# Local blocks with probability transposes in the score banks, one front stage, and early middle norms

## The chip, the cores and the metric

The kernel runs on one core of a Trainium2 chip. The metric is the device time of one execution in microseconds. TensorE (PE) multiplies, VectorE (DVE), ScalarE (ACT) and GpSimd (POOL) compute, and SyncE (SP) issues the loads and stores. The profiler records one execution; its granted TensorE clock is a mean of the two levels 1.2 and 2.4 GHz (1.00 is 2.4).

## What is computed

Two transformer layers on x of 2 x 2048 x 128 in float32, each an attention block and a local block, both added to x under adaptive layer norms whose shift, scale and gate come from a conditioning vector:

```python
mods = silu(c) @ w_mod                      # six vectors of 128 for each layer and batch
# layer 0 attention: delta-rule memory over 4096 rows, chunks of 64, k normalised per head
# layer 1 attention: causal linear attention, 64 features, then its own feed-forward
for layer in local_block:                   # layer 0: 6 layers, 16 heads, window 32; layer 1: 2, 8, 64
    q, k, v = split(shift(x) @ Wqkv)
    q, k = rotary(l2norm(q)), rotary(l2norm(k))
    x = x + softmax(mask(8 q k'), own and previous window) v @ Wo
    a, g = split(layernorm(shift(x)) @ W1 + b1)      # 341 wide
    x = x + (a * gelu(g)) @ W2 + b2
```

The gate of the modulation is kept away from zero: magnitude at least 0.25 with its sign.

## The kernel before

The stages run one behind the other, each a block of five instruction streams (one for each engine) that wait for each other by semaphores: `zero_rows` stores two zero rows, `modulation_stage` makes `mods`, `delta_attention_stage` is the first attention, then the feed stage, `local_block_stage` for layer 0 (758 to 4124 us), `linear_block_stage` (4126 to 4330), `local_block_stage` for layer 1 (4330 to 5240) and the residual.

**The local block** works on 16 row tiles of 128 for each batch and layer: 192 tiles in layer 0 and 64 in layer 1, in a software pipeline. Every engine runs `emit(k, T, hf)` once for each half of the heads `hf`; a loop body holds two tiles, so a pair of tiles has four halves. They are called A (T even, hf 0), B (T even, hf 1), C (T odd, hf 0) and D (T odd, hf 1) here. In each half TensorE projects q and k of one tile (L1539), transposes them (L1574) and the attention output of an earlier one (L1593), projects values (L1611), transposes probabilities (L1626), writes masks (L1662) and scores (L1670) of another tile, and multiplies probabilities by values (L1691, in layer 1 L1693). Beside that, A has the up projections (L1719), of which the first parts fill gate banks and the third part factor banks; B and D the output projection (L1640) and the transpose of the input (L1650); C the feature transposes (L1703) and the down projection (L1731). ScalarE copies out of PSUM (L1808 qkT, L1816 outT, L1842 values, L1857 probabilities), and has exponentials (L1849), the gelu gates (L1914) with a table load ahead (L1928) and behind (L1933). VectorE makes softmax maxima and differences, the attention output (L1982), the rotary products and `hidden` (L2062).

The eight PSUM banks: two for projections `ps_q`, two for transposes `ps_t`, two for scores `ps_s`, two for attention outputs `ps_o`. NS is 2 in layer 0 and 1 in layer 1. Scores use columns 0 to 255 of each score bank. The probability transposes write to `ps_t[2 - NS]`; the values, feature transposes and down projection share `ps_x = ps_t[NS - 1]`, in layer 0 the other transpose bank. Waits on a count held in a register take instructions of their own on an engine's sequencer ahead of the instruction that waits.

**The front.** `modulation_stage` loads weights and vectors, makes silu, has 8 matmul calls of 384 columns, and then six VectorE operations of 128 columns for each of eight slices (L155 to L161). `delta_attention_stage` then loads x, weights and tables (L216 to L222), VectorE takes statistics of 32 tiles (L87) and roots, modulates eight groups (L99 to L103), and after the projections (L248) ScalarE copies k (L279); VectorE waits for all 32 copies and then takes squares and their sums in two parts (L310, L311).

**The linear block** has eight groups of four tiles. Its first loop does the attention and ends with `xm` (L1111), its second the feed-forward: statistics (L1053), roots, `normalise_mid` (L941 on ScalarE), transposes, `affine` (L981), up projections (L928), gelu, down projections (L918). VectorE's second loop begins three groups ahead of TensorE's.

Of the kernel before, what the change touches and what calls it, by code (L numbers as in the profile page):

```python
# [105 lines left out]
def modulation_stage(nc, mods, c_rows, w_mod):  # L106

    with ExitStack() as ctx:
        sb = lambda n, shape, dt=F32: ctx.enter_context(nc.sbuf_tensor(f"mod_{n}", shape, dt))
        sem = ctx.enter_context(stage_semaphores(nc, "mod"))  # L110
        c = sb("c", [128, 4])
        e = sb("e", [128, 4])
        silu = sb("silu", [128, 4])
        wide = sb("wide", [128, 4, 128])
        w = sb("w", [128, 2, 768])
        sign = sb("sign", [128, 128])
        mag = sb("mag", [128, 128])
        ps = [[ctx.enter_context(nc.psum_tensor(f"mod_ps{k}{j}", [128, 512], F32)) for j in range(2)] for k in range(4)]
        loaded, exped, wide_done, product, seq = sem("loaded"), sem("exped"), sem("wide_done"), sem("product"), sem("seq")
        with nc.Block() as block:  # L120
            @block.sync
            def _(sp):
                for l in range(2):
                    sp.dma_start(w[:, l, :], w_mod[l]).then_inc(loaded, 16)
                    for b in range(2):
                        sp.dma_start(c[:, 2 * l + b:2 * l + b + 1], c_rows[l][b, :].rearrange("(p o) -> p o", o=1)).then_inc(loaded, 16)

            @block.scalar
            def _(act):
                act.wait_ge(loaded, 96)  # L130
                nc.scalar.activation(e[:, :], c[:, :], ACT.Exp, scale=-1.0).then_inc(exped, 1)

            @block.tensor
            def _(pe):
                pe.wait_ge(loaded, 96)
                pe.wait_ge(wide_done, 1)
                for k in range(4):
                    for j in range(2):
                        last = nc.tensor.matmul(ps[k][j][:, 0:384], wide[:, k, :], w[:, k // 2, 384 * j:384 * j + 384], start=True, stop=True)
                last.then_inc(product, 1)  # L140

            @block.vector
            def _(dve):
                step = Steps(dve, seq)
                dve.wait_ge(exped, 1)
                step(nc.vector.tensor_scalar(e[:, :], e[:, :], 1.0, None, ALU.add))
                step(nc.vector.reciprocal(e[:, :], e[:, :]))
                step(nc.vector.tensor_tensor(silu[:, :], e[:, :], c[:, :], ALU.mult))
                nc.vector.tensor_copy(wide[:, :, :], silu[:, :].rearrange("p (k o) -> p k o", o=1).to_broadcast([128, 4, 128])).then_inc(wide_done, 1)
                dve.wait_ge(product, 1)  # L150
                for k in range(4):
                    for j in range(2):
                        src = ps[k][j]
                        out = mods[:, k, 3 * j:3 * j + 3, :]
                        step(nc.vector.tensor_copy(out[:, 0, :], src[:, 0:128]))  # L155
                        step(nc.vector.tensor_scalar(out[:, 1, :], src[:, 128:256], 1.0, None, ALU.add))

                        step(nc.vector.tensor_scalar(sign[:, :], src[:, 256:384], 0.0, 2.0, ALU.is_ge, ALU.mult))
                        step(nc.vector.tensor_scalar(mag[:, :], src[:, 256:384], -1.0, 0.25, ALU.mult, ALU.max))
                        step(nc.vector.scalar_tensor_tensor(mag[:, :], src[:, 256:384], 0.25, mag[:, :], ALU.max, ALU.max))  # L160
                        step(nc.vector.scalar_tensor_tensor(out[:, 2, :], sign[:, :], -1.0, mag[:, :], ALU.add, ALU.mult))  # L161


def delta_attention_stage(nc, x_dram, xr, mods, w_qkvT, w_oT, alpha_raw, beta_raw, tables, qkv_dram):
# [3 lines left out]
    with ExitStack() as ctx:  # L168
# [9 lines left out]
        with ExitStack() as c2:  # L178
            sb = lambda n, shape, dt=F32: c2.enter_context(nc.sbuf_tensor(f"da_{n}", shape, dt))
            ps = [c2.enter_context(nc.psum_tensor(f"da_psa{i}", [128, 512], F32)) for i in range(8)]  # L180
# [12 lines left out]
            alpha, beta = sb("alpha", [128, H]), sb("beta", [128, H])  # L193
            loaded, seq, h_ready, hT_ps, hT_done = (sem(n) for n in ("loaded", "seq", "h_ready", "hT_ps", "hT_done"))
# [17 lines left out]
            with nc.Block() as block:  # L212
                @block.sync
                def _(sp):
                    for b in range(2):
                        sp.dma_start(xr[:, 16 * b:16 * b + 16, :], x_dram[b].rearrange("(t p) d -> p t d", p=128)).then_inc(loaded, 16)  # L216
# [16 lines left out]

                @block.tensor
                def _(pe):
                    pe.wait_ge(loaded, 144)
# [899 lines left out]
def local_block_stage(nc, name, depth, heads, window, x, x_rows, mid_rows, v_rows, weights, tables):  # L1136
# [18 lines left out]
    with ExitStack() as ctx:  # L1155
# [205 lines left out]
        with nc.Block() as block:  # L1361
# [161 lines left out]
            def _(pe):  # L1523

                def project(k, T, hf, s):

                    t, h = item(T, hf, AT_PROJ)
                    if live(k, t):
                        j = NS * h + s
                        pe.wait_ge(S["xT_done"], tiles_(k, t))  # L1530
                        if s == 0:
                            pe.wait_ge(wq_in[h], reloads(k, t, 16))
# [744 lines left out]
```

## Time and profile before

| | us |
|---|---|
| median of 3 runs | 5260.22 |
| lowest and highest | 5258.66, 5263.18 |
| profiled execution | 5259.56 |
| its span | 5257.8 |
| TensorE busy in the span | 4656.7 (89%) |
| VectorE, ScalarE, GpSimd busy | 3876.4, 3195.5, 2753.1 |
| mean granted clock | 0.954 |

The profiled execution's own time is 1.8 us above its span. A time line row gives the start in us from the span's start, the length, the engine, the source line, the operation, and in brackets the idle time of the engine just before it with what ended it. Consecutive instructions of a kind are one row; matmuls in float32 appear as two each.

### The profile page before, as it was taken

The numbers are of one execution on the slowest core, as the hardware profiler recorded it, in microseconds if no ns is written. First come the engines' busy times: TensorE is split into PE (matmuls) and PEld (weight loads), VectorE is DVE, ScalarE is ACT, GpSimd is POOL, SyncE is SP. The second block draws the span as 40 slices with busy tenths as digits, with TensorE's granted clock in tenths as the row PEclk, the third lists the DMA queues.
The fourth block names the chain that finished last, engine by engine and source line by source line (L and its number), as shares of the span: only waits on it lengthen the run. The fifth ranks groups of instructions, "written<-read, shape, count | busy, mean of one in ns | idle before, by whom it ended". The sixth has DMA issues, their size and how long they took to land. (4 is left out here: it accounts for less than half of the span.)

```text
span 5257.8 us, 220614 instructions
## 1 busy us (share of the span) xinstructions
PE 4656.7 (89%) x81616; PEld 3372.6 (64%) x81616; DVE 3876.4 (74%) x8260; ACT 3195.5 (61%) x6716; POOL 2753.1 (52%) x3917
## 2 busy tenths in 40 slices
PE   3558948999999999999999999999999576999996
PEld 2556736676767666676767666767676454666665
DVE  5984567777777777777777777777777566777775
ACT  1002526677777777677777677777776344777675
POOL 0004116666666666666666666666665325555552
PEclk6996979999999999999999999999999688999998
DMA  1000125554545454555454555455554003444442
GB/s 58 17 1 18 43 57 130 137 132 134 132 130 139 127 143 127 141 131 141 128 141 128 140 131 140 129 136 133 138 134 119 17 7 87 115 113 114 114 113 77
DMA packets 704914, 564.32 MB, mean 107 GB/s; under 512 B 223492, under 2 KB 629864, under 8 KB 704008
## 3 DMA queue, kind: packets, MB, share of 16 engines
q1 hardware_dynamic: 691080, 537.36, 38.5%
q10 hardware_dynamic: 13312, 22.02, 1.3%
q14 instruction: 441, 3.61, 0.2%
q8 instruction: 81, 1.33, 0.1%
HBM read 359.38 MB, written 200.02 MB: 106 GB/s over the span
## 5 line engine op out<-in xcount | busy, mean ns | idle before, releaser
L2134 POOL TENSOR_TENSOR L_qk<-L_cos_part,L_sin_part 128x512 f32<-128x512 f32 x896 | 1128.7, 1273 | 151.5 <-DVE L_sin_part L2012 151.0
L1797 ACT ACTIVATE L_squares<-L_ps_q 128x512 f32<-128x512 f32 x896 | 534.8, 597 | 929.2 <-PE L_ps_q L1539 922.6
L1539 PE MATMUL L_ps_q<-L_w_qkv,L_xT 128*128 128x512 f32 x1792 | 971.9, 625 | 30.0 <-DVE L_sin_part L2012 11.1
L2125 POOL TENSOR_TENSOR L_qk<-L_qk,L_rnorm 128x1024 f32<-128x1024 f32 (+1 forms) x512 | 864.0, 1688 | 17.8 <-POOL L_rnorm L2108 0.5
L1574 PEld LDWEIGHTS L_ps_t<-L_ident,L_qk 128*128 128x128 f32 x3584 | 446.1, 141 | 479.1 <-issue 374.5
L2011 DVE TENSOR_TENSOR L_cos_part<-L_ps_q,L_rot 128x512 f32<-128x512 f32 x896 | 611.0, 682 | 41.2 <-POOL L_rot L2144 31.2
L2012 DVE TENSOR_TENSOR L_sin_part<-L_ps_q,L_rot 128x512 f32<-128x512 f32 x896 | 610.9, 682 | 0.0
L2013 DVE TENSOR_REDUCE L_sumsq<-L_squares 128x8 f32<-128x512 f32 x896 | 606.7, 677 | 0.0
L2102 POOL TENSOR_TENSOR L_nw_a<-L_rnorm 128x32 f32<-128x32 f32 (+1 forms) x256 | 59.5, 232 | 993.7 <-ACT L_rnorm L1827 993.7
L1574 PE MATMUL L_ps_t<-L_ident,L_qk 128*128 128x128 f32 x3584 | 540.2, 274 | 4.4 <-POOL L_qk L2125 3.2
L1808 ACT ACTIVATE L_qkT<-L_ps_t 128x512 f32<-128x512 f32 x896 | 530.6, 592 | 15.8 <-PE L_ps_t L1574 15.7
L1640 PE MATMUL L_ps_q<-L_w_out,L_outT 128*128 128x128 f32 x3584 | 446.8, 277 | 2.6 <-ACT L_outT L1816 1.7
L1626 PEld LDWEIGHTS L_ps_t<-L_ident,L_probs 128*128 128x128 f32 x2048 | 218.9, 141 | 333.7 <-issue 262.4
L1640 PEld LDWEIGHTS L_ps_q<-L_w_out,L_outT 128*128 128x128 f32 x3584 | 423.7, 193 | 4.3 <-issue 4.0
L1670 PE MATMUL L_ps_s<-L_qkT 64*32 64x64 f32 (+1 forms) x26624 | 401.8, 226 | 0.2 <-ACT L_qkT L1808 0.2
L1611 PE MATMUL L_ps_t<-L_w_qkv,L_xT 128*128 128x512 f32 x768 | 393.4, 594 | 0.6 <-issue 0.6
L1996 DVE TENSOR_TENSOR L_probs<-L_ps_s,L_neg_max 128x512 f32<-128x512 f32 x512 | 354.3, 692 | 53.6 <-DVE L_neg_max L1991 0.5
L1977 DVE RECIPROCAL L_p_rec<-L_ps_o 128x8 f32<-128x8 f32 (+1 forms) x512 | 102.9, 201 | 359.9 <-PE L_ps_o L1691 288.7
L1982 DVE TENSOR_TENSOR L_att<-L_ps_o,L_p_rec 128x512 f32<-128x512 f32 (+1 forms) x512 | 320.1, 625 | 54.3 <-DVE L_p_rec L1977 1.4
L1670 PEld LDWEIGHTS L_ps_s<-L_qkT 64*32 64x32 f32 (+1 forms) x26624 | 357.9, 107 | 0.3 <-issue 0.3
L1626 PE MATMUL L_ps_t<-L_ident,L_probs 128*128 128x128 f32 x2048 | 324.7, 281 | 28.5 <-issue 16.2
L1991 DVE TENSOR_REDUCE L_neg_max<-L_ps_s 128x8 f32<-128x512 f32 (+1 forms) x512 | 349.0, 682 | 0.2 <-PE L_ps_s L1670 0.2
(290 smaller groups left out, 8908.2 us busy)
## 6 DMA issues: line engine op xcount, KB each, us to landing
L_val<-v_rows SPq DMA_DIRECT2D x896, 260.0 KB, 3.8
v_rows<-L_val SPq DMA_DIRECT2D x384, 260.0 KB, 2.1
v_rows<-L_val SPq DMA_DIRECT2D x512, 65.0 KB, 2.0
L_rot_base<-in_rot SPq DMA_DIRECT2D x256, 128.0 KB, 2.1
v_rows<-L_val SPq DMA_DIRECT2D x128, 130.0 KB, 2.1
L_x_in<-x_rows SPq DMA_DIRECT2D x512, 32.0 KB, 1.7
mid_rows<-z SPq DMA_DIRECT2D x256, 64.0 KB, 1.6
L_f_in<-mid_rows SPq DMA_DIRECT2D x256, 64.0 KB, 2.0
```

Of the source, the lines that this page charges most:

```text
L1539: nc.tensor.matmul(ps_q[j % 2][:, :], xT[:, parity(t), :], w_qkv[:, 0:2, 256 * j:256 * j + 256], start=True, stop=True).then_inc(S["proj_p ...
L1574: last = nc.tensor.transpose(ps_t[0][:, 128 * i:128 * i + 128], qk[:, parity(t), h, s, 128 * i:128 * i + 128], ident[:, :])
L1626: last = nc.tensor.transpose(ps_t[2 - NS][:, 128 * i:128 * i + 128], probs[:, h, 128 * i:128 * i + 128], ident[:, :])
L1640: last = nc.tensor.matmul(ps_q[0][:, 0:128], outT[:, u, :], w_out[:, u, :], start=(u == 0), stop=(u == U - 1))
L1670: last = nc.tensor.matmul(S_VIEW[W * a:W * a + W, p, i, :], qkT[rows, 0, u, W + W * a:2 * W + W * a], qkT[rows, kk, u, W * a:W * a + 2 * W ...
L1797: nc.scalar.activation(squares[:, j % 2, :], ps_q[j % 2][:, :], ACT.Square).then_inc(S["sq_done"], 1)
L1808: nc.scalar.activation(dst, ps_t[0][:, :].rearrange("x (a u q) -> x a u q", a=2, u=2), ACT.Copy).then_inc(S["qkT_done"], 1)
L2011: nc.vector.tensor_tensor(R4(cos_part[:, j % 2, :]), qkp, cs[:, :, 0, :, :, :].to_broadcast([128, 2, 4, 2, 32]), ALU.mult)
L2012: nc.vector.tensor_tensor(R4(sin_part[:, j % 2, :]), qkp[:, :, :, ::-1, :], cs[:, :, 1, :, :, :].to_broadcast([128, 2, 4, 2, 32]), ALU.mul ...
L2013: nc.vector.tensor_reduce(sumsq[:, t % 2, j, :], squares[:, j % 2, :].rearrange("x (g d) -> x g d", g=8), AX.X, ALU.add).then_inc(S["ss_do ...
L2125: nc.gpsimd.tensor_tensor(v, v, r, ALU.mult).then_inc(S["normed"], 1)
L2134: nc.gpsimd.tensor_tensor(qk[:, t % 2, h, s, :], cos_part[:, j % 2, :], sin_part[:, j % 2, :], ALU.add).then_inc(S["added"], 1)
```

## The change

**Local blocks.** The probability transposes go to `P_VIEW`, columns 256 to 511 of the two score banks, and wait only for `shifted` (VectorE has read the scores), the exponentials and their values. Scores wait, ahead of the masks, for the copy of the probabilities of the same half (`pT_done`), for `att_done` and `qkT_done`, and the waits of the next half's projection are put ahead of the masks too (`ready_to_project`). Between masks and scores nothing waits, nor ahead of the weighted values, except in A for `fact_done`. In layer 0 the down projection's result goes to `ps_q[0]`, and the order in C is probability transposes, down projection, feature transposes. In layer 1 the order in C is feature transposes, probability transposes, down projection; the third part of the up projections waits for `oT_done` in place of `pT_done` (in layer 0 for `qkT_done`), and ScalarE copies the probabilities ahead of the gelu table load.

**Front.** `zero_rows` and `modulation_stage` become part of `delta_attention_stage`: its queue first loads what modulation needs, then x, weights and tables, then stores the zero rows. ScalarE copies shifts and scales (two operations of 128x1024), VectorE makes the gates in four operations of 128x1024 behind the statistics. The first part of k's squares waits for 16 copies instead of 32.

**Linear block.** Statistics, roots and `normalise_mid` of groups 0 to 2 move to turns i = 5, 6, 7 of the first loop (`EARLY_MID`); VectorE's second loop starts at group 0.

```diff
 def delta_attention_stage(...):
...
-                    act.wait_ge(loaded, 144)
+                    act.wait_ge(mod_in, 96)
+                    nc.scalar.activation(c_exp[:, :], c_in[:, :], ACT.Exp, scale=-1.0).then_inc(exped, 1)
+                    act.wait_ge(product, 1)
+                    by_part = mods[:, :, :, :].rearrange("p k (j i) d -> p (k j) i d", i=3)
+                    nc.scalar.activation(by_part[:, :, 0, :], banks[:, :, 0:128], ACT.Copy).then_inc(mods_done, 1)
+                    nc.scalar.activation(by_part[:, :, 1, :], banks[:, :, 128:256], ACT.Copy, bias=1.0).then_inc(mods_done, 1)
+                    act.wait_ge(loaded, 112)
...
+                    dve.wait_ge(x_in, 32)
                     group_stats(nc, dve, step, xr, mean, rstd, (st, mv, var, half, tmp))
+                    dve.wait_ge(mods_done, 2)
+                    raw = banks[:, :, 256:384]
+                    nc.vector.tensor_scalar(sign, raw, 0.0, 2.0, ALU.is_ge, ALU.mult).then_inc(mods_done, 1)
...
-                    dve.wait_ge(k_out, SUB)
...
                     for j in range(2):
+                        dve.wait_ge(k_out, SUB // 2 * (j + 1))
...
 def linear_block_stage(...):
...
+                    if i - 5 in EARLY_MID:
+                        normalise_mid(i - 5)
...
+                    early = i - 5
+                    if early in EARLY_MID:
+                        dve.wait_ge(S["mid_done"], early + 1)
+                        statistics(4, four(xm, early))
+                    if live(i + 1) or live(i + 3) or early in EARLY_MID:
+                        roots(0, i + 3, 0 if live(i + 1) else 4, 8 if live(i + 3) or early in EARLY_MID else 4, S["roots_a"])
...
-                for g in range(-3, NG + 1):
+                for g in range(NG + 1):
...
 def local_block_stage(...):
...
+        ps_d = ps_q[0][:, 0:256] if NS == 2 else ps_x[:, 256:512]
...
+        P_VIEW = ps_s[:, :, 256:512].rearrange("x b (i q) -> x b i q", i=2)
...
+                def ready_to_project(k, T, hf):
+
+                    t, h = item(T, hf, AT_PROJ)
+                    if live(k, t):
+                        pe.wait_ge(wq_in[h], reloads(k, t, 16))
+                        wait(pe, S["rotated"], steps_(k, t, NS * h - 2))
...
-                        wait(pe, S["pT_done"], halves(k, t, h - 1))
+                        read, g = item(T, hf, AT_SOFTMAX)
+                        if live(k, read):
+                            pe.wait_ge(S["shifted"], halves(k, read, g))
                         pe.wait_ge(S["exp_done"], halves(k, t, h))
                         for i in range(4):
-                            last = nc.tensor.transpose(ps_t[2 - NS][:, 128 * i:128 * i + 128], probs[:, h, 128 * i:128 * i + 128], ident[:, :])
+                            last = nc.tensor.transpose(P_VIEW[:, i // 2, i % 2, :], probs[:, h, 128 * i:128 * i + 128], ident[:, :])
...
-                        wait(pe, S["shifted"], halves(k, t, h - 1))
+                        v, g = item(T, hf, AT_PV)
+                        if live(k, v):
+                            pe.wait_ge(S["pT_done"], halves(k, v, g))
+                            wait(pe, S["att_done"], halves(k, v, g - 1))
+                        else:
+                            wait(pe, S["shifted"], halves(k, t, h - 1))
+                        pe.wait_ge(S["qkT_done"], steps_(k, t, NS * h + NS - 1))
                         wait(pe, S["kprev_done"], count(k, t, 1, 0))
...
-                        pe.wait_ge(consts_in, CONSTS)
-                        pe.wait_ge(S["qkT_done"], steps_(k, t, NS * h + NS - 1))
...
-                        pe.wait_ge(S["pT_done"], mine)
-                        wait(pe, S["att_done"], before)
...
                         feature_transposes(k, T)
-                        down_projection(k, T)
...
                     prob_transposes(k, T, hf)
+                    if goes_down and early:
+                        down_projection(k, T)
...
                     if goes_down and not early:
+                        down_projection(k, T)
                         feature_transposes(k, T)
-                        down_projection(k, T)
+                    ready_to_project(k, T + hf, 1 - hf)
                     scores(k, T, hf)
...
                         exponentials(k, T, hf)
+                        if NS == 1:
+                            prob_copy(k, T, hf)
                         if live(k, T - TO_UP):
                             nc.scalar.preload_act_table_set("gelu_and_others")
-                        prob_copy(k, T, hf)
+                        if NS == 2:
+                            prob_copy(k, T, hf)
```

TensorE, layer 0, the end of half B and the whole of half C, before (REGISTER_ALU is a sequencer instruction of a wait):

```order
L60 REGISTER_ALU
L1662 MATMUL L_ps_s<-L_masks,L_ident_bf 32x256 x8
L1670 MATMUL L_ps_s<-L_qkT 32x64 x32
L1691 MATMUL L_ps_o<-L_val,L_probsT 32x65 x32
L1539 MATMUL L_ps_q<-L_w_qkv,L_xT 128x512
...
L1611 MATMUL L_ps_t<-L_w_qkv,L_xT 128x512
L1626 MATMUL L_ps_t<-L_ident,L_probs 128x128 x4
L60 REGISTER_ALU
L1703 MATMUL L_ps_t<-L_ident,L_f_norm 128x128 x2
L1731 MATMUL L_ps_t<-L_w_down,L_hidden 128x128 x6
L1662 MATMUL L_ps_s<-L_masks,L_ident_bf 32x256 x8
L1670 MATMUL L_ps_s<-L_qkT 32x64 x32
```

and the same place after:

```order
L1663 REGISTER_ALU
L60 REGISTER_ALU
L1669 MATMUL L_ps_s<-L_masks,L_ident_bf 32x256 x8
L1675 MATMUL L_ps_s<-L_qkT 32x64 x32
L1698 MATMUL L_ps_o<-L_val,L_probsT 32x65 x32
...
L1614 MATMUL L_ps_t<-L_w_qkv,L_xT 128x512
L1627 MATMUL L_ps_s<-L_ident,L_probs 128x128 x4
L60 REGISTER_ALU
L1747 MATMUL L_ps_q<-L_w_down,L_hidden 128x128 x6
L60 REGISTER_ALU
L1710 MATMUL L_ps_t<-L_ident,L_f_norm 128x128 x2
L1669 MATMUL L_ps_s<-L_masks,L_ident_bf 32x256 x8
```

The probability transposes changed their bank, one more sequencer instruction stands ahead of B's masks, and the feature transposes moved behind the down projection.

ScalarE, linear block, the end of the first loop, before:

```order
L966 ACTIVATE la_low<-la_low 128x512
L954 ACTIVATE la_k_tok<-la_p_kt 128x256
L958 ACTIVATE la_attT<-la_p_t 128x512 x2
L941 ACTIVATE la_y_n<-la_xm,la_shift,la_rstd 128x128 x12
L981 ACTIVATE la_y_T<-la_p_t,la_ln 128x512
```

and after:

```order
L971 ACTIVATE la_low<-la_low 128x512
L925 ACTIVATE la_y_n<-la_xm,la_shift,la_rstd 128x128 x4
L959 ACTIVATE la_k_tok<-la_p_kt 128x256
L963 ACTIVATE la_attT<-la_p_t 128x512 x2
L932 ACTIVATE la_y_T<-la_p_t,la_ln 128x512
```

The twelve operations between the last copy of attT and the first affine are gone from there; the last four of them now stand ahead of it, the others in the two turns before.

## Rows read from the trace of the kernel before

**Rows 1.** Local blocks: stretch, length, busy PE, PEld, DVE, ACT, POOL, clock, DMA, GB/s.

```profile
758.00:4124.00 3366.00, 3261.45 (x66432) 2312.85 (x66432) 2584.73 (x5184) 2347.64 (x4799) 2135.92 (x2808) 0.99 0.50 132
...
4330.00:5240.00 910.00, 792.90 (x7985) 571.31 (x7983) 621.37 (x1462) 605.23 (x1389) 462.25 (x829) 0.97 0.38 104
```

**Rows 2.** Time line of TensorE, layer 0, half C: start us, us, engine, line, operation.

```profile
2010.97 1.02 PE L1611 MATMUL L_ps_t<-L_w_qkv,L_xT 128*128 128x512 f32 x2
2012.05 0.63 PE L1626 MATMUL L_ps_t<-L_ident,L_probs 128*128 128x128 f32 x4
...
2013.05 1.50 PE L1731 MATMUL L_ps_t<-L_w_down,L_hidden 128*128 128x128 f32 x12
2014.48 0.30 PE L1662 MATMUL L_ps_s<-L_masks,L_ident_bf 64*32 64x256 bf16 x8
...
2015.24 0.85 PE L1691 MATMUL L_ps_o<-L_val,L_probsT 64*32 64x65 f32 x64
2016.10 1.10 PE L1539 MATMUL L_ps_q<-L_w_qkv,L_xT 128*128 128x512 f32 x2
```

**Rows 3.** Time line, layer 0, half B and the start of half C.

```profile
1999.60 1.12 PE L1539 MATMUL L_ps_q<-L_w_qkv,L_xT 128*128 128x512 f32 x2
...
2005.75 0.58 ACT L1857 ACTIVATE L_probsT<-L_ps_t 128x512 f32<-128x512 f32 x1
2006.29 0.30 PE L1662 MATMUL L_ps_s<-L_masks,L_ident_bf 64*32 64x256 bf16 x8
...
2007.06 0.85 PE L1691 MATMUL L_ps_o<-L_val,L_probsT 64*32 64x65 f32 x64
2007.85 1.12 PE L1539 MATMUL L_ps_q<-L_w_qkv,L_xT 128*128 128x512 f32 x2
2009.00 0.60 ACT L1797 ACTIVATE L_squares<-L_ps_q 128x512 f32<-128x512 f32 x1 [2.33 <-PE L_ps_q L1539]
```

**Rows 4.** Time line, layer 0, the end of half A and the start of B.

```profile
2033.67 1.12 PE L1539 MATMUL L_ps_q<-L_w_qkv,L_xT 128*128 128x512 f32 x2
...
2034.38 0.69 DVE L1982 TENSOR_TENSOR L_att<-L_ps_o,L_p_rec 128x512 f32<-128x512 f32 x1
...
2035.21 0.63 PE L1593 MATMUL L_ps_t<-L_ident,L_att 128*128 128x128 f32 x4
```

**Rows 5.** Time line, layer 1, half A, then half B.

```profile
4703.19 1.13 PE L1719 MATMUL L_ps_t<-L_f_normT,L_w_up 128*128 128x256 f32 x4 [0.98 <-ACT L_probsT L1857]
...
4709.84 0.30 PE L1662 MATMUL L_ps_s<-L_masks,L_ident_bf 64*64 64x256 bf16 x4
...
4710.18 0.57 ACT L1857 ACTIVATE L_probsT<-L_ps_t 128x512 f32<-128x512 f32 x1
4710.85 0.71 PE L1693 MATMUL L_ps_o<-L_val,L_probsT 128*64 128x65 f32 x16 [0.27 <-issue]
```

**Rows 6.** Waits, layer 1, 4450 to 5150 us: total, times, longest.

```profile
PE L_ps_t L1719 <- ACT L_probsT L1857: 26.0, 27, 1.1
```

**Rows 7.** Time line of the front, 0 to 110 us.

```profile
34.20 0.29 DVE L161 SCALAR_TENSOR_TENSOR mods<-mod_sign,mod_mag 128x128 f32<-128x128 f32 x1
35.46 2.87 SPq L216 DMA_DIRECT2D xr<-in_L_attn_x  x2
...
47.31 0.87 DVE L87 BATCH_NORM_STATS2 da_st<-xr 128x6 f32<-128x128 f32 x4 [12.83 <-DMA da_beta<-in_L_attn_beta_raw]
...
63.62 1.12 DVE L99 TENSOR_SCALAR da_h<-xr,da_mean,da_rstd 128x128 f32<-128x128 f32 x4
...
109.44 2.29 DVE L310 TENSOR_TENSOR da_prod<-da_ks 128x2048 f32<-128x2048 f32 x1 [24.61 <-ACT da_ks L279]
```

**Rows 8.** Time line of the linear block, between its two loops.

```profile
4265.21 0.69 DVE L1111 TENSOR_TENSOR la_xm<-la_p_v,la_xm 128x512 f32<-128x512 f32 x1 [2.59 <-PE la_p_v L893]
...
4269.71 1.65 ACT L941 ACTIVATE la_y_n<-la_xm,la_shift,la_rstd 128x128 f32<-128x128 f32 x4 [5.75 <-DVE la_shift L1064]
...
4285.83 2.05 PE L928 MATMUL la_p_qk<-la_y_T,la_w_f 128*128 128x512 f32 x2 [13.30 <-ACT la_y_T L981]
```

More of the change, by code:

```diff
@@ L103, in modulated_group @@
     nc.vector.tensor_tensor(out, out, vec(0), ALU.add).then_inc(done, 1)
[L106 to L161, printed above, removed]
@@ L179, in delta_attention_stage @@
             sb = lambda n, shape, dt=F32: c2.enter_context(nc.sbuf_tensor(f"da_{n}", shape, dt))
-            ps = [c2.enter_context(nc.psum_tensor(f"da_psa{i}", [128, 512], F32)) for i in range(8)]
+            banks = c2.enter_context(nc.psum_tensor("da_psa", [128, 8, 512], F32))
+            ps = [banks[:, i, :] for i in range(8)]
             hT = sb("hT", [128, 4096])
@@ L235, in _ @@
                 def _(pe):
-                    pe.wait_ge(loaded, 144)
+                    pe.wait_ge(mod_in, 96)
+                    pe.wait_ge(wide_done, 1)
+                    for k in range(4):
+                        for j in range(2):
+                            last = nc.tensor.matmul(ps[2 * k + j][:, 0:384], wide[:, k, :], w_m[:, k // 2, 384 * j:384 * j + 384], start=True, stop=True)
+                    last.then_inc(product, 1)
+                    pe.wait_ge(loaded, 112)
+                    pe.wait_ge(mods_done, 6)
                     for g in range(8):
@@ L781, in linear_block_stage @@
         PHASES = NG + 5
+        EARLY_MID = range(3)
         rstd, shift = sb("rstd", [128, 2, PHASES, 8]), sb("shift", [128, 2, PHASES, 8])
@@ L1564, in qk_transposes @@
                         elif NS == 2:
-                            wait(pe, S["pT_done"], halves(k, t - 1, h - 1))
+                            wait(pe, S["qkT_done"], steps_(k, t, j - 1))
                             if hf == 1 and parity(T) == TO_UP % 2:
@@ L1587, in out_transposes @@
                         else:
-                            pe.wait_ge(S["pT_done"], halves(k, t, h))
+                            wait(pe, S["oT_done"], halves(k, t, h - 1))
                             if hf == 1 and parity(T) == TO_UP % 2:
@@ L1682, in weighted_values @@
                             wait(pe, S["fact_done"], gated)
-                        pe.wait_ge(S["pT_done"], mine)
-                        wait(pe, S["att_done"], before)
+                        s, _ = item(T, hf, AT_SCORE)
+                        if not live(k, s):
+                            pe.wait_ge(S["pT_done"], mine)
+                            wait(pe, S["att_done"], before)
                         for i in range(HU):
```

122 lines of the change are left out of this document (70 added, 52 removed).

## Prediction

> **What bounds the kernel now.** I read the busy times by stage first. Layer 0's local block takes 3366 us of the span and TensorE is busy for 3261 of them at a granted clock of 0.99; layer 1's takes 910 us with 793 busy [rows 1]. Both other engines that matter, VectorE and ScalarE, are busy for 2585 and 2348 us of the first block, so there TensorE is the engine to shorten, but only where no other engine ends the wait last. So I then read one pair of tiles as a time line. A pair has four halves: A (up projections, gelu gates), B (output projection), C (feature transposes, down projection), D (output projection). In layer 0 one pair, from half B's first projection to the next one's, is 34.07 us [rows 3, 4], and 96 pairs make the block; layer 1 has 32. A saving of 0.1 us in a pair is 10 us of the total in layer 0 and 3 us in layer 1. Last I read the front (time 0 to 110) and the seam in the middle of the linear block, where TensorE idles and a chain of other engines sets the time.
>
> **Layer 0, half C.** From the values' first matmul to the probability transposes' first stand 1.08 us [rows 2]. The two matmuls themselves need about 0.86 (0.43 each), so 0.22 is a wait: the transposes go to bank ps_t0, which ScalarE is still copying the last qkT from. Behind them the feature transposes wait for the copy of the values. From the first probability transpose to the masks pass 2.43 us for 18 small matmuls (4, 2 and 12); the 12 of the down projection alone take 1.43 with the step to the masks, at most 0.12 each, so 18 need 2.14 and 0.29 is wait. After the change the probability transposes go to the free half of the score banks, the down projection to a projection bank, and the feature transposes come last, when the values' copy is long done. Both waits go: 0.51, and I take -0.50. What is late next is the copy of the probabilities, which the masks now wait for: in this half it has the 18 matmuls to hide in, so it costs nothing.
>
> **Layer 0, half D** loses the wait before the probability transposes only. Between nothing and C's 0.22 I take -0.10, since its neighbours are less crowded.
>
> **Layer 0, the seams.** At the end of a half TensorE's sequencer works off waits on registers between the last weighted-value matmul and the next projection. From the weighted values to the projection pass 0.86 us after C and 0.79 after B, which has one such instruction less [rows 2, 3]: 0.07 each. The new order puts these waits ahead of the masks, where they cost the same but partly lie under a wait. One instruction goes after B, one after D and three after C: 0.35 if all counts. I take -0.25, because half D then starts with transposes of the attention output that cannot run earlier than VectorE makes it.
>
> **Layer 0, half A to B** gains nothing: VectorE ends the attention output at 2035.07 and TensorE's transposes of it start at 2035.21 [rows 4]. Whatever TensorE saves in A it waits there. Between nothing and the 0.51 of half C, I take 0.
>
> **Layer 0, half B** pays. The masks start at 2006.29, the ScalarE copy of the probabilities ends at 2006.33, and the weighted values, the copy's reader, start at 2007.06 behind the masks and scores [rows 3]. So today 0.77 us of masks and scores run beside the copy. Now the masks write to the same banks from which the copy reads, and wait for it. The three to five sequencer instructions between that wait and the masks, at 0.07 each, add 0.21 to 0.35. Masks start at about 2006.33 + 0.33 = 2006.66, so +0.37. The bounds are 0 (the ScalarE chain in B moves up by what C and D save) and 0.77 (nothing hides any more).
>
> Sum for a pair: -0.50 - 0.10 - 0.25 + 0 + 0.37 = -0.48; with 96 pairs -46, bounds +35 (only B's loss stays) and -115 (no loss in B, A gains 0.35 as well: -1.20 each).
>
> A rule of the Trainium skill speaks against this change (page "Perfetto Trace Analysis", section "Matmuls"): independent matmul groups should rotate through different PSUM banks so that the evacuation of one overlaps the next. By that rule B's 0.77 is lost whole, in each half where the copy ends late. The trace agrees for B only; in C the copy is hidden.
>
> **Layer 1** is worse off. In half B masks start at 4709.84, and the copy ends at 4710.18 + 0.57 = 4710.75, the weighted values start at 4710.85 [rows 5]. After the change masks start at about 4710.75 + 0.28 = 4711.03, and the weighted values 0.67 later (masks and scores; the 4710.85 before was itself held by the copy), so at 4711.70 to 4711.85: +0.85 to +1.0. In C and D the order of steps changes: probability transposes go ahead of the down projection, which hides the copy, and one wait less at the seams: -0.15 together. In half A the last up projections now wait 0.98 us for the copy, 27 times for 26.0 us in 27 pairs [rows 5, 6]. That wait goes, but the gelu gates that follow are held by the table load and their own queue on ScalarE, so it is worth 0; the copy moves ahead of the table load, which puts the gates up to 0.15 later. Sum +0.87 (0.88 + 0.15 - 0.16), times 32: +28. Bounds: +10 (part of A's 0.98 does come through) and +38 (B at +1.19, the masks' full delay).
>
> **Front.** Modulation is a stage of its own now: VectorE ends its last small operation there at 34.49, and only then are x and the weights loaded. VectorE starts the statistics at 47.31 and the first group of rows at 63.62 [rows 7]. In one stage the loads of x are issued right after six modulation loads. From the issue at 35.46 to the landing of everything pass 11.85 us, so x is there by 4 + 10 = 14, the statistics (16.3 us) end at 30.4, beside them matmuls and two ScalarE copies are long done, and four VectorE operations of 128x1024 follow (half of the 2.29 us that 128x2048 took, so 4 x 1.2 = 5). Groups start at 35.4: -28. The squares of k are now started after half of the projections: one product and one reduction of 2.29 us each [rows 7] fall into the 24.61 us in which VectorE waits: -4.6. Sum -33. Bounds -20 (x lands only after 22) and -36.
>
> **Linear block.** xm of the last group is done at 4265.21 + 0.69; statistics, roots and normalisation follow, group 0's normalisation starts at 4269.71 and the first up projection only at 4285.83, since ScalarE normalises three groups ahead of the first affine [rows 8]. With groups 0 to 2 normalised in the first loop, the up projection follows xm at 4265.9 by a transpose and an affine, about 1.2 us: 4267, so 18.8 earlier. The first loop pays: statistics and roots of one group are 3.8 us together (4265.90 to 4269.71), and two turns get the statistics alone, the third both; GpSimd's work on the groups, now beside it, stretches VectorE. VectorE idles 2.59 us before that last xm, but is waited for elsewhere in the turn; between 3.8 (once) and 11.4 (three times whole) I take 7. -12; bounds -5 and -18.
>
> **Sum**: -46 + 28 - 33 - 12 = -63 from the profiled run's 5259.56 gives 5196.6; the median of the runs is 0.7 above it, so 5197.
>
> **Rivals.**
> (a) *VectorE and ScalarE pace the pair.* What C, D and the seams save is given back as wait in A to B, where the row already shows it [rows 4], and B's wait of the masks for the copy stays. Price 96 x 0.37 = +36, layer 1 +28, front -33, linear -12: +19, 5279. It decides where a pair of layer 0 gets longer by more than 17 / 96 = 0.18 us. Against it: TensorE is busy 97% of the block [rows 1], and ScalarE idles 2.33 us for TensorE at the start of half C [rows 3]. By the Trainium skill's rule above ("Perfetto Trace Analysis", section "Matmuls") this would be the case with 0.77 in B instead of 0.37, +57: 5317.
> (b) *No gain and no loss in layer 0* (saving and price in B cancel): +28 - 33 - 12 = -17, 5243.
> (c) *TensorE's sum comes through.* The copies in B come earlier by what the other halves gain, since ScalarE's chain there starts when TensorE gives it work: layer 0 -115, layer 1 +10: -150, but with half of the step in B still paid, -0.37 / 2 x 96 less: -132, 5128.
> (d) *The front does not overlap*: the loads of x share the queue with modulation's small ones and land late; -10 in place of -33: 5220.
>
> **How the numbers follow.** Forecast 0.50 (own range 5170 to 5225), (a) 0.12, (b) 0.13, (c) 0.15, (d) 0.10. The time is the forecast's. The range must leave out no more than 0.2: it takes in (b), (d) and half of (c), from 5135 to 5245. A measurement of this kernel tells 0.2% (10.5 us) from no change: above 5270.7 is slower, and (a) holds most of it (0.10); same, 5249.7 to 5270.7, gets 0.05, the edge between (a) and (b); faster 0.85.
>
> **What the next profile would show.** Right: in C the probability transposes follow the values by 0.86 to 0.9 us and the masks come 2.15 after them; in B the masks start 0.3 to 0.4 after the copy's end and the weighted values 0.77 after that; a pair of layer 0 takes 33.6; in layer 1 half B is about 1 us longer and the wait of the up projections for the copy is gone; the first group of rows starts at 35; the first up projection of the linear block stands 1 to 2 us behind the last xm. Wrong: a pair of layer 0 at 34.1 or more with longer waits of TensorE for VectorE (a, b); at 33.2 or less (c); x landing after 20 (d).

## The result, and the profile after

The changed kernel takes 5230.05 us (median of 5 runs, 5227.24 to 5233.27) against 5260.09 for the kernel before in the same comparison: a ratio of 0.9944, 95% interval 0.9930 to 0.9959. It is 30 us faster; the forecast was 63 us. The profiled execution has a span of 5231.0 us, 26.8 less than before, at the same mean clock of 0.954.

The span divides by the first and last instruction of each stage on TensorE, VectorE or ScalarE (the moves are rounded after the subtraction):

| stage | before | after | moved | forecast |
|---|---|---|---|---|
| front, to the end of the first attention | 709.3 | 677.2 | -32.1 | -33 |
| layer 0, local block | 3372.7 | 3341.8 | -30.9 | -46 |
| linear block | 249.7 | 239.1 | -10.5 | -12 |
| layer 1, local block | 856.4 | 903.7 | +47.3 | +28 |

The four moves sum to -26.2. Of the 37 us that the forecast has too much, 19 are layer 1's and 15 layer 0's. Busy times of the two local blocks after the change, to be read against [rows 1] (stretch, length, busy us of PE, PEld, DVE, ACT, POOL, clock, DMA share, GB/s):

```profile
718.00:4060.00 3342.00, 3159.07 (x66432) 2342.38 (x66432) 2575.38 (x5192) 2338.52 (x4800) 2138.34 (x2808) 0.99 0.50 133
...
4308.00:5213.00 905.00, 762.25 (x7808) 561.11 (x7808) 596.13 (x1352) 584.57 (x1344) 436.53 (x808) 0.97 0.37 103
```

For layer 1 the second row of [rows 1] is the wrong one to compare with. Its stretch begins at 4330, but the linear block runs to 4376 and layer 1's block starts only at 4382: 7985 matmuls lie in it instead of the block's 7808. The same block before the change, by its own ends, is:

```profile
4382.00:5239.00 857.00, 762.22 (x7808) 548.85 (x7808) 592.82 (x1352) 583.60 (x1344) 435.75 (x808) 0.98 0.39 108
```

TensorE is busy for the same 762 us there, so the 47 us that the block grew are idle time of TensorE.

In layer 0 TensorE is now busy 94.5% of the block, 97% before: its busy time fell by 102 us for the same 66432 matmuls, the block by 31. The ends of matmuls are modelled in a profile, so the 102 are not read as work saved. What counts is that idle time has come in, and two views show where. The first is TensorE in layer 0, half C, then half B, as a time line:

```profile
1999.08 1.12 PE L1541 MATMUL L_ps_q<-L_w_qkv,L_xT 128*128 128x512 f32 x2
...
2002.21 1.02 PE L1614 MATMUL L_ps_t<-L_w_qkv,L_xT 128*128 128x512 f32 x2
2003.07 0.60 PE L1627 MATMUL L_ps_s<-L_ident,L_probs 128*128 128x128 f32 x4
...
2005.16 0.30 PE L1669 MATMUL L_ps_s<-L_masks,L_ident_bf 64*32 64x256 bf16 x8
...
2006.67 1.13 PE L1541 MATMUL L_ps_q<-L_w_qkv,L_xT 128*128 128x512 f32 x2
...
2023.67 1.13 PE L1541 MATMUL L_ps_q<-L_w_qkv,L_xT 128*128 128x512 f32 x2
...
2025.56 0.63 PE L1596 MATMUL L_ps_t<-L_ident,L_att 128*128 128x128 f32 x4 [0.33 <-DVE L_att L2004]
...
2031.29 0.30 PE L1669 MATMUL L_ps_s<-L_masks,L_ident_bf 64*32 64x256 bf16 x8 [0.61 <-ACT L_probsT L1875]
...
2032.78 1.12 PE L1541 MATMUL L_ps_q<-L_w_qkv,L_xT 128*128 128x512 f32 x2
```

From one half C to the next are 33.70 us, where a pair took 34.07 [rows 3, 4]. In C the probability transposes follow the values by 0.86 (1.08 in [rows 2]), and the masks come 2.09 after them (2.43); from the masks to the next projection pass 1.51 (1.62). In B TensorE idles 0.61 us ahead of the masks, for the copy of the probabilities. ScalarE in the same half:

```profile
2028.88 0.86 ACT L1911 ACTIVATE L_f_norm<-L_f_in,L_f_b,L_f_r 128x128 f32<-128x128 f32 x2
...
2030.17 0.58 ACT L1875 ACTIVATE L_probsT<-L_ps_s 128x512 f32<-128x512 f32 x1
```

The copy ends at 2030.75 and the masks start at 2031.29, 0.54 later. Before the change the masks started 0.04 ahead of the copy's end [rows 3]. The trace also holds the instructions of TensorE's sequencer (register arithmetic and semaphore waits), which a time line leaves out. Five of them lie in this gap, starting at 2030.78, 2030.89, 2031.00, 2031.09 and 2031.18: the released wait for the copy and four behind it, one every 0.10 us.

The halves' medians, from projection to projection, over some 85 pairs of layer 0 (1000 to 3900 us) and 25 of layer 1:

| half | layer 0 before | after | layer 1 before | after |
|---|---|---|---|---|
| A | 9.37 | 9.06 | 7.72 | 7.95 |
| B | 8.25 | 9.13 | 5.97 | 6.99 |
| C | 8.28 | 7.60 | 5.89 | 5.78 |
| D | 8.18 | 7.93 | 5.52 | 5.54 |

In layer 1's half B the masks wait for the copy as well. They start 0.40 behind its end and the weighted values 1.07 behind it, where the weighted values started 0.10 behind it [rows 5]:

```profile
4651.63 0.57 ACT L1875 ACTIVATE L_probsT<-L_ps_s 128x512 f32<-128x512 f32 x1
...
4652.60 0.30 PE L1669 MATMUL L_ps_s<-L_masks,L_ident_bf 64*64 64x256 bf16 x4 [1.02 <-issue]
...
4653.27 0.73 PE L1700 MATMUL L_ps_o<-L_val,L_probsT 128*64 128x65 f32 x16
```

In the front VectorE starts the statistics at 15.71 and the first group at 36.98, which were 47.31 and 63.62 [rows 7]:

```profile
15.71 0.87 DVE L87 BATCH_NORM_STATS2 da_st<-xr 128x6 f32<-128x128 f32 x4 [7.68 <-DMA xr<-in_L_attn_x]
...
32.00 1.22 DVE L272 TENSOR_SCALAR da_prod<-da_psa 128x1024 f32<-128x1024 f32 x1
...
36.98 1.11 DVE L99 TENSOR_SCALAR da_h<-xr,da_mean,da_rstd 128x128 f32<-128x128 f32 x4
```

In the linear block the first up projection starts 1.78 us after the start of the last xm, where it started 20.62 after it [rows 8]; the first loop up to that xm takes 147.28 us instead of 138.97:

```profile
4210.50 0.69 DVE L1102 TENSOR_TENSOR la_xm<-la_p_v,la_xm 128x512 f32<-128x512 f32 x1 [3.22 <-PE la_p_v L877]
4212.28 2.05 PE L912 MATMUL la_p_qk<-la_y_T,la_w_f 128*128 128x512 f32 x2 [0.96 <-ACT la_y_T L932]
```

### The profile page after: what moved, and what is told of

Same layout as the page of the kernel before. It is cut to its first block and busy times, and to the rows that moved or that the text cites. A ratio compares the mean times of both kernels' runs of the same rounds, so it can differ in the third digit from the quotient of the medians.

```text
span 5231.0 us, 219416 instructions
## 1 busy us (share of the span) xinstructions
PE 4561.0 (87%) x81616; PEld 3422.0 (65%) x81616; DVE 3847.0 (74%) x8190; ACT 3188.2 (61%) x6718; POOL 2757.7 (53%) x3917
## 5 line engine op out<-in xcount | busy, mean ns | idle before, releaser
L2033 DVE TENSOR_TENSOR L_cos_part<-L_ps_q,L_rot 128x512 f32<-128x512 f32 x896 | 609.5, 680 | 40.6 <-POOL L_rot L2167 32.1
L1627 PEld LDWEIGHTS L_ps_s<-L_ident,L_probs 128*128 128x128 f32 x2048 | 250.0, 142 | 223.5 <-issue 220.3
L1698 PE MATMUL L_ps_o<-L_val,L_probsT 64*32 64x65 f32 x24576 | 340.8, 227 | 30.2 <-DVE L_hidden L2084 18.5
```

The source lines that it names most:

```text
L2033: nc.vector.tensor_tensor(R4(cos_part[:, j % 2, :]), qkp, cs[:, :, 0, :, :, :].to_broadcast([128, 2, 4, 2, 32]), ALU.mult)
```

## Experiments: do the parts add?

**front_only** is the kernel before with the changed first attention stage.

```diff
-        zero_rows(nc, (x_rows, mid_rows), t["zeros"])
-        modulation_stage(nc, mods, [t["L0_c"], t["L1_c"]], [t["L0_wmod"], t["L1_wmod"]])
+        delta_attention_stage(..., (x_rows, mid_rows), ...)
```

> The kernel before with the change's front stage alone. Theory (parts add): the first attention ends at 677 instead of 709 us, the local blocks and the linear block keep 3373, 250 and 856 us, total 5260 - 32 = 5228. Rival (an interaction): another stage moves by more than 5 us.

One run took 5236.1 us. The first attention ends at 679.4; layer 0 has 3369.1, the linear block 252.9 and layer 1 863.2. The front's part is its own. Layer 1's block stands 6.8 us above the profile of before though nothing in it changed. By the letter that meets the expectation's rival (another stage moves by more than 5 us); one run can't tell whether it is an interaction or the block's own spread, so a difference of 7 us in a single profile of that block is read as nothing here.

**linear_only** is the kernel before with the changed linear block.

```diff
+        EARLY_MID = range(3)
...
-                for g in range(-3, NG + 1):
+                for g in range(NG + 1):
```

> The kernel before with the change's linear block alone. Theory (the early middle norms take 18.9 us out of the seam between the two loops, and cost part of it back in the first loop): the linear block takes 237 to 241 instead of 250 us, first loop 4 to 10 us longer, all other stages as before, total 5250. Rival (the gain needs the earlier stages' timing): block within 3 us of 250.

One run took 5249.81 us, the linear block 237.0 instead of 249.7, and layer 0 kept 3371.1. The last xm starts 1.77 us ahead of the first up projection, as in the changed kernel. This part adds too, to within the 2 us by which the block is shorter here.

**l1_old** keeps everything changed but layer 1's local block, which is the one of before.

```diff
-        local_block_stage(nc, "L1", 2, 8, 64, ...)
+        local_block_stage_old(nc, "L1", 2, 8, 64, ...)
```

> The changed kernel with layer 1's local block as before; front, linear block and layer 0 stay changed. Theory (the miss in layer 1 is the block's own, from the masks' wait and the gates): the time from layer 1's first to its last instruction returns from 903.7 to about 856 us, the total to 5230 - 47 = 5183. Rival (part of layer 1's loss comes from what stands ahead of it, an earlier start or another clock): the block stays above 880 and the total above 5205.

Measured: 5192.49 us (ratio to before 0.9874, 0.9857 to 0.9890), layer 1's block 862.4. Most of the loss in layer 1 belongs to its block: 37.6 us between the medians, 41 of 47 between the profiles' blocks. The other 6 stay with the old block. Its half A takes 11.95 and 12.28 us at two turns of the layer loop, where the kernel before takes 9.36 and 9.34, and VectorE stands still twice in a row there:

```profile
4675.77 0.18 DVE L3048 RECIPROCAL L_p_rec<-L_ps_o 128x4 f32<-128x4 f32 x1 [2.48 <-issue]
4678.16 0.42 DVE L3053 TENSOR_TENSOR L_att<-L_ps_o,L_p_rec 128x256 f32<-128x256 f32 x1 [2.21 <-issue]
```

Idle time put down to "issue" is time for which the profile shows no wait. So 5.5 us of layer 1's loss do not come from the new block: the rival's mechanism is there in this small part, with the block far below its 880.

**l0_old** is the reverse, layer 0's block as before.

```diff
-        local_block_stage(nc, "L0", 6, 16, 32, ...)
+        local_block_stage_old(nc, "L0", 6, 16, 32, ...)
```

> The changed kernel with layer 0's local block as before. Theory (layer 0 alone brought 31 us): layer 0's block returns from 3341.8 to 3373 us, total about 5261. Rival (the blocks interact): it stays within 15 us of 3342.

One run took 5255.4 us; layer 0 has 3368.4, layer 1 900.0. Layer 0's part brings 25 to 31 us and layer 1 loses 40 to 47 whatever stands ahead. At those two turns the new block of layer 1 has one standstill of 3.5 us here, not two.

## Experiments: what holds the masks in half B

**wait_last** moves one wait.

```diff
                         if live(k, v):
-                            pe.wait_ge(S["pT_done"], halves(k, v, g))
                             wait(pe, S["att_done"], halves(k, v, g - 1))
...
                         pe.wait_ge(S["qkT_done"], steps_(k, t, NS * h + NS - 1))
                         wait(pe, S["kprev_done"], count(k, t, 1, 0))
+                        if live(k, v):
+                            pe.wait_ge(S["pT_done"], halves(k, v, g))
                         pe.sem_inc(S["pe_turn"], 1)
```

> One line moved, in both blocks: the masks' wait for the copy of the probabilities stands behind the other waits instead of ahead of them, directly before the last sequencer instruction ahead of the masks. Theory (between the end of the copy and the masks pass 0.54 us in layer 0's half B because three to five sequencer instructions follow that wait): the gap falls to 0.1 to 0.25, layer 0 gains 0.3 x 96 = 29 us, layer 1 0.25 x 32 = 8, total about 5193. Rival (the gap is the time in which TensorE gets back to work after a wait, or the other waits end last): gap above 0.45, total 5225 to 5235.

Measured: 5184.18 us (0.9855, 0.9838 to 0.9871), 46 us below the changed kernel. Layer 0's block is 3301.3 (-40.5), layer 1's 894.6 (-9.1). Half B of layer 0 on both engines:

```profile
2017.96 0.59 ACT L1876 ACTIVATE L_probsT<-L_ps_s 128x512 f32<-128x512 f32 x1
...
2018.64 0.30 PE L1670 MATMUL L_ps_s<-L_masks,L_ident_bf 64*32 64x256 bf16 x8 [0.17 <-issue]
```

The copy ends at 2018.55 and the masks start 0.09 later, not 0.54. Median B fell from 9.13 to 8.68, and the 0.45 of 96 pairs is 43 us. That is more than the 29 us expected. So the gap was made of the other waits and their sequencer instructions, which followed this wait. In the trace the same four now start at 2016.83 to 2017.12, beside the output projection. Only the last of them, which now carries the wait for the copy too, holds, until 2018.59. What stands ahead of that wait costs nothing. The rival (a fixed time for getting back to work) falls.

**bd_bank** sends the probability transposes of B and D of layer 0 to the transpose bank of before, so that their masks need no copy. The waits for the copy and for `att_done` go back to their old place behind the scores, and the transposes get the waits of before.

```diff
+                        own = NS == 2 and hf == 1
...
-                            last = nc.tensor.transpose(P_VIEW[:, i // 2, i % 2, :], probs[...], ident[:, :])
+                            last = nc.tensor.transpose(ps_t[0][:, 128 * i:128 * i + 128] if own else P_VIEW[:, i // 2, i % 2, :], probs[...], ident[:, :])
...
-                        if live(k, v):
+                        if live(k, v) and not (NS == 2 and hf == 1):
                             pe.wait_ge(S["pT_done"], halves(k, v, g))
```

> In layer 0 the probability transposes of halves B and D go to the transpose bank with the waits of before, so the masks there need not wait for the copy; A and C stay changed. Theory (the wait of masks for the copy costs half B 0.5 to 0.6 us): masks stand beside the copy again, B falls from 9.13 to 8.6, D stays within 0.1 of 7.93 or loses its 0.1, layer 0 gains 35 to 55 us, total 5175 to 5195. Rival (ScalarE and VectorE pace halves A and B whatever TensorE waits for): what B gains, A loses, layer 0 within 15 us of 3342, total 5215 to 5235.

Measured: 5195.37 us (0.9880, 0.9864 to 0.9897), layer 0's block 3307.8 (-34), both at the edge of what was expected. The masks stand beside the copy again:

```profile
2015.37 0.58 ACT L1881 ACTIVATE L_probsT<-L_ps_t 128x512 f32<-128x512 f32 x1
...
2015.96 0.30 PE L1675 MATMUL L_ps_s<-L_masks,L_ident_bf 64*32 64x256 bf16 x8
```

B falls to 8.61 and D rises from 7.93 to 8.08, A stays at 9.06. The shared banks, with the waits that they bring, cost B 0.52 us and gain D 0.15. What B gains is not lost in A, so VectorE and ScalarE do not take it back. This run takes two things away at once, the shared bank and the wait with its sequencer instructions behind it, and wait_last separates them: there the banks are still shared and B takes 8.68. The sharing by itself is thus worth 0.07 us in B, and the order of the waits 0.45.

**fnorm_late** shortens what stands ahead of the copy on ScalarE, in half B of both blocks.

```diff
                         val_copy(k, T, hf)
-                        if hf == 1 and T % 2 == TO_LN % 2:
-                            normalised(k, T)
                         exponentials(k, T, hf)
                         prob_copy(k, T, hf)
+                        if hf == 1 and T % 2 == TO_LN % 2:
+                            normalised(k, T)
```

> The changed kernel with one move on ScalarE, in half B of both blocks: the two normalisations of the feed-forward input stand behind the exponentials and the copy of the probabilities instead of ahead of them. Theory (what holds the masks in half B is the end of ScalarE's queue, 5.21 to 7.09 us into the half, of which the two normalisations are 0.77): the copy ends 0.77 earlier at about 6.3, then TensorE's own work (input transpose starting at 6.74, then the sequencer's waits) ends last; masks start at 6.95 to 7.1 instead of 7.63, layer 0 gains 0.5 to 0.65 x 96 = 48 to 62 us, layer 1 0.5 x 32 = 16, total 5155 to 5170. Rival (the normalisations, now later, hold half C's feature transposes, or the exponentials' input comes no earlier): under 15 us in all, total above 5215.

Measured: 5151.93 us (0.9793, 0.9776 to 0.9810), 78 us below the changed kernel, 3 below the expected band. Layer 0's block is 3280.5 (-61), layer 1's 883.0 (-21).

```profile
2008.67 0.59 ACT L1875 ACTIVATE L_probsT<-L_ps_s 128x512 f32<-128x512 f32 x1
2009.15 0.87 ACT L1911 ACTIVATE L_f_norm<-L_f_in,L_f_b,L_f_r 128x128 f32<-128x128 f32 x2
...
2009.88 0.30 PE L1669 MATMUL L_ps_s<-L_masks,L_ident_bf 64*32 64x256 bf16 x8
```

The copy now ends 0.62 us ahead of the masks, which follow TensorE's own work, and the late normalisations delay nobody: C stays at 7.60. B is 8.45, 0.68 less. So of B's 9.13 us 0.68 stood above TensorE's own work: 0.45 for the order of the waits, the rest, 0.23, because ScalarE's queue ended the copy late. Either move takes the 0.45, because a copy that ends 0.62 early hides the same instructions.

## Experiments: layer 1's half A, and a version that beats both

**l1_table** puts layer 1's copy of the probabilities behind the gelu table load again.

```diff
                         exponentials(k, T, hf)
-                        if NS == 1:
-                            prob_copy(k, T, hf)
                         if live(k, T - TO_UP):
                             nc.scalar.preload_act_table_set("gelu_and_others")
-                        if NS == 2:
-                            prob_copy(k, T, hf)
+                        prob_copy(k, T, hf)
```

> The changed kernel with layer 1's copy of the probabilities behind the gelu table load again, as it was before the change. Theory (half A of layer 1 got 0.26 us longer since that copy, now ahead of the table load, has to wait for the transposes and holds the load and the gates): gates 0.16 to 0.3 earlier, layer 1's block gains 5 to 9 us, from 903.7 to about 897. Rival (the masks, which now wait for the copy, start later than the gates allow, and the order was needed): the block is 5 us or more longer.

Measured: 5221.25 us (0.9932, 0.9916 to 0.9949). Its interval overlaps that of the changed kernel (0.9930 to 0.9959), so the 9 us between the medians are not clear of noise by themselves. The profile shows the effect: half A takes 7.68 instead of 7.95, below the 7.72 of before, which is 8.6 us in 32 pairs, and the block 891.1 instead of 903.7. ScalarE in half A, the changed kernel first, then this run:

```profile
4642.55 0.60 ACT L1875 ACTIVATE L_probsT<-L_ps_s 128x512 f32<-128x512 f32 x1 [0.16 <-PE L_ps_s L1627]
4643.17 1.28 ACT L1949 ACT_TABLE_LOAD   x1
4644.46 1.19 ACT L1933 ACTIVATE L_gate<-L_ps_o,L_b_up 128x256 f32<-128x256 f32 x3
```

```profile
4660.95 1.28 ACT L1947 ACT_TABLE_LOAD   x1
4662.24 0.60 ACT L1875 ACTIVATE L_probsT<-L_ps_s 128x512 f32<-128x512 f32 x1
4662.73 1.18 ACT L1933 ACTIVATE L_gate<-L_ps_o,L_b_up 128x256 f32<-128x256 f32 x3
```

The copy ahead of the load waits 0.16 us for its transposes. The load then starts only when the copy has ended, while gates behind a copy start 0.11 before its end. Together the gates come 0.26 us later, counted from the exponentials.

**best1** takes the changed front, linear block and layer 0 with both moves of half B, and layer 1 as before the change: the edits of wait_last and fnorm_late in the new block, and the call of l1_old.

> Changed front, linear block and layer 0, with the masks' wait moved to the last place and the normalisations behind the copy in layer 0; layer 1's block as before the change. If the effects add: 5230 - 41 (layer 1 as before) - 40 (wait moved) - 10 to 30 (normalisations later, of which the moved wait has taken a part) = 5120 to 5140. Rival (VectorE and ScalarE pace the pair by now): above 5145.

Measured: 5134.28 us (0.9764, 0.9748 to 0.9780). Layer 0's block is 3276.8, 3.7 below that of the late normalisations alone: half B takes 8.45 in both. Once the copy ends ahead of TensorE's own work, the place of its wait makes no difference that can be seen.

**best2** has all three moves, the edits of wait_last, fnorm_late and l1_table, in the new block of both layers and no old block.

> The changed kernel with three moves, in both local blocks: the masks' wait for the copy last, ScalarE's normalisations behind the copy in half B, and in layer 1 the copy behind the gelu table load. Theory (the three act on different waits): layer 0 as in the last combined kernel, 3277; layer 1 from 903.7 by 20.7 (normalisations), up to 9 (wait moved) and 12.6 (table load): 861 to 870, the same as layer 1's block before the change (856 to 867). Total 5125 to 5140. Rival (with the copy behind the table load, the masks of layer 1's half A wait for it again, once B has stopped being the brake): layer 1 above 880, total above 5145.

Measured: 5131.69 us over 5 runs (0.9761, 0.9746 to 0.9775), 98 us below the changed kernel and 129 below the one before. The blocks in its profile:

```profile
716.00:3996.00 3280.00, 3158.38 (x66432) 2343.98 (x66432) 2578.37 (x5192) 2338.58 (x4800) 2135.34 (x2808) 0.99 0.51 136
4244.00:5108.00 864.00, 755.67 (x7808) 556.19 (x7808) 597.68 (x1352) 583.18 (x1344) 435.46 (x808) 0.97 0.39 107
```

Layer 1's halves are 7.68, 5.88, 5.78 and 5.40, each below the one of before, 0.36 a pair in all or 11 us in 32 pairs; yet the block is 863.7, 7.3 above the profile of before and within the spread of the old block (856.4 to 867.1 in five profiles). Two places take the gain back. The first 16 halves of the block, where the pipeline fills, take 94.4 us instead of 90.8, and the two turns of the layer loop 22.5 instead of 18.7. The two combined kernels cannot be told apart.

## Why the prediction was wrong

The direction, the stages and, for the most part, what each change does to its wait were right, and the time lies in the range (5135 to 5245); the gain was forecast at twice its size, because two terms were priced too low: half B of layer 0 and the block of layer 1. By the steps of the sum:

- **Front, -33**: -32.1. x landed at 15.7 instead of 14, which gave back 1.7; the four operations took 5.0, and the groups start 26.6 earlier and not 28. The squares of k brought 5.7 instead of 4.6.
- **Linear block, -12**: -10.5. The seam gave 18.84 as worked out (18.8), the first loop cost 8.3 and not 7.
- **Half C, -0.50, and D, -0.10**, with -0.25 for the seams: C gave 0.68 and D 0.25, 0.93 together against 0.85. Right, slightly low. The seams can't be read from the first weighted value any more, since that one now starts among the scores. From the masks to the next projection the medians fell by 0.05 in B, 0.11 in C and 0.16 in D, 0.32 together, near the 0.35 that the prediction named if all counts; ahead of the masks C gained 0.56 and D 0.09.
- **Half A to B, 0**: A is 0.31 shorter and the transposes of the attention output start 0.34 later in B. The sum is +0.03. Right, and for the reason given: VectorE ends that wait in both kernels. The masks of A are 0.50 earlier; 0.20 of that goes where the weighted values now wait for VectorE's `hidden`.
- **Half B, +0.37, failed.** Beyond the 0.34 passed on from A, B lost 0.54. The term for the sequencer was mis-sized: 0.21 to 0.35 for three to five instructions at 0.07 each, where the gap measured 0.54. The trace has five in the gap, and they start 0.10 us apart. The 0.07 was the difference between two seams of the kernel before, one with two such instructions and one with three, where they run beside the last weighted values; their own steps there are 0.09 to 0.14, so the difference of the seams showed less than one of them costs. The run with the wait moved shows those it passed to be worth 0.45 together. In 96 pairs the error of 0.17 is 16 us. C and D gave 8 us more than forecast, which hid half of it by luck; the medians' sum of -0.36 is -35 us in 96 pairs and -31 in the block, whose first and last tiles are not such pairs.
- **Layer 1, +28, failed**, beyond its own bound of 38. B lost 1.02 instead of 0.88, mostly by the same term: the gap behind the copy is 0.40, not 0.28. A lost 0.23 instead of 0.15, and C and D gave back 0.09 instead of 0.16: +1.16 in the medians, 37 us. A's term was mis-sized, for the copy ahead of the table load costs its wait for the transposes and a seam with the load; with the copy behind the load (l1_table) the whole loss of A is gone. The block's length was also misread: the 910 us and 793 busy of [rows 1] hold 52 us from before the block. The sum did not use it. The last 10 us are no step of the sum, which put at nothing what is not a pair in full swing. At two turns of the layer loop half A takes 12.8 and 13.3 us (9.4 before), 7.4 together; the remaining 3 are not assigned. VectorE stands still at the turns, put down to issue, twice in a row:

```profile
4693.48 0.18 DVE L1999 RECIPROCAL L_p_rec<-L_ps_o 128x4 f32<-128x4 f32 x1 [2.43 <-issue]
4695.89 0.42 DVE L2004 TENSOR_TENSOR L_att<-L_ps_o,L_p_rec 128x256 f32<-128x256 f32 x1 [2.23 <-issue]
4696.37 0.44 PE L1596 MATMUL L_ps_t<-L_ident,L_att 128*128 128x128 f32 x2 [3.28 <-DVE L_att L2004]
```

  Before, the first of the two was there alone, at 2.37. The second does not belong to layer 1's code. It is there in all eight runs with the changed layer 0, l1_old and best1 with their old block of layer 1 among them. In the four with the old layer 0 it is missing: before, front_only, linear_only, and l0_old with the changed block of layer 1. By what means layer 0's block brings it about stays open.

The rule that was set against the change (the Trainium skill, page "Perfetto Trace Analysis", section "Matmuls": rotate independent groups through different banks) names the right place, since B is where the change loses. As a price it was further off than the forecast: by it B loses 0.77, and 0.54 was lost in layer 0, where the forecast had 0.37; its time of 5317 is 87 us above the measured one, the forecast's 33 below. And of the 0.54 the runs give 0.07 to the sharing itself and 0.45 to the order of the waits. With the copy 0.77 us earlier on its own engine the same shared banks cost nothing that can be seen.

Rival (a), that VectorE and ScalarE give back what TensorE saves, holds for A to B only. That B's masks keep waiting for ScalarE's copy, which it also said, is what the trace shows; the range took (a)'s time out, and rightly.

## What to carry to other kernels

When a wait is added ahead of work that a copy of another engine releases, look first at what stands ahead of the copy in its engine's queue and does not belong there; here moving two normalisations of 0.86 us was worth 61 us in one block. Then put that wait behind all others: here the sequencer instructions behind the wait that ended last were paid in full, and ahead of it they were free. The two remedies overlap: both together gave 3.7 us more in that block than the first alone. Price such instructions from their own starts in the trace, not from the difference of two seams. And before you blame a shared bank, restore it and move the wait in separate runs; here most of the loss was the order of the waits.

## What the runs showed of the hardware that was not expected

- The waits and sequencer instructions of `att_done`, `qkT_done` and `kprev_done`, all fulfilled by then, cost 0.45 us behind a wait that ends last (one start every 0.10 us) and nothing ahead of it, where two seams had differed by 0.07.
- VectorE's two issue stalls in a row at a turn of a loop, 2.43 and 2.23 us, where the kernel before had one of 2.37. They come and go with the block that ran ahead, also where the block that has them is unchanged.
- The same block of layer 1, unchanged, took 856.4, 860.3, 862.4, 863.2 and 867.1 us in five profiles. The second stall explains most of it in two of them: at the two turns 5.5 us of the 6.0 in 862.4 (l1_old), and 7.7 of the 10.7 in 867.1 (best1). The other two have no second stall and are 3.9 and 6.8 above the lowest; so much of a stage one profile leaves open.
